# Wider key projections in a second attention layer, paired maxima and shifts, and row scaling on ScalarE

## The reference

```python
x = x + L0_xattn(ctx, layernorm(x), ctx, ...)        # 16 heads of 64, causal
x = x + L0_ffn(layernorm(x), gate, up, down)         # FP4-quantised, width 352
x = x + L1_xattn(layernorm(x), ctx, Wq, Wk, Wv, Wk_ip, Wv_ip, Wo, bo)
x = x + L1_ffn(layernorm(x), router, 8 experts, top 2)

# L1_xattn: two softmaxes over two segments of the keys, the outputs added
q = (x @ Wq);  k = ctx[:, :77] @ Wk;  k_ip = ctx[:, 77:] @ Wk_ip    # v, v_ip alike
out = softmax(q k^T / 8) v + softmax(q k_ip^T / 8) v_ip
out = out @ Wo + bo
```

## Time and profile before

| | us |
|---|---|
| median of 3 runs | 664.25 (664.08 to 667.1) |
| the profiled execution | 667.46 |
| its span, first to last instruction | 665.7 |
| first step of the second layer (scores of n = 64) | 248.3 |
| scores of n = 126 | 540.7 |
| VectorE copies the first expert's weights | 552.6 |
| mean granted TensorE clock | 0.978 |

### The profile page before, as it was taken

The page is one execution under the profiler, slowest core; times in us unless marked ns, Lnnn a source line. Parts: engine busy times, 40 slices in busy tenths (PEclk is TensorE's granted clock), DMA queues, the critical chain, the costliest instruction groups (busy, mean ns, idle before and its releaser), DMA issues.

```text
span 665.7 us, 16842 instructions
## 1 busy us (share of the span) xinstructions
PE 617.7 (93%) x5833; PEld 568.2 (85%) x5833; DVE 492.1 (74%) x1370; ACT 461.8 (69%) x1397; POOL 309.8 (47%) x444
## 2 busy tenths in 40 slices
PE   5898999999999999999999999999999987998990
PEld 5787888898888899999989989889888976988990
DVE  6578676586886869888898896888675675674654
ACT  5988999998888986656565656665663545665762
POOL 4365354354434444444444352445336575565550
PEclk9999999999999999999999999999897999998995
DMA  9800000000000000346654060000000001212215
GB/s 226 256 2 1 1 2 1 2 1 3 1 1 1 3 17 2 127 95 126 114 118 91 2 159 1 2 1 1 1 6 28 26 25 47 64 57 65 77 49 198
DMA packets 49612, 33.36 MB, mean 50 GB/s; under 512 B 9508, under 2 KB 46088, under 8 KB 49528
## 3 DMA queue, kind: packets, MB, share of 16 engines
q1 hardware_dynamic: 47256, 27.61, 16.8%
q0 software_dynamic: 2272, 4.67, 2.1%
HBM read 17.64 MB, written 14.63 MB: 48 GB/s over the span
## 4 chain that ended last, share of the span: by engine, by line
PE 64%; ACT 11%; issue 9%; POOL 7%; DVE 4%; DMA 3%; SPq 0%; POOLq 0%; DVEq 0%; ACTq 0%
PE ps_h L812 7%; PE ps_j L590 7%; PE ps_s L759 7%; ACT scores L987 7%; PE ps_t L797 6%; PE ps_h L829 6%; PE ps_j L369 5%; PE ps_j L371 4%; PE ps_j L370 4%; PE ph L1717 4%; PE py L1728 4%; POOL probs L1531 3%; POOL xs_scratch L1642 2%; PE pf L620 2%; PE pf L677 1%
## 5 line engine op out<-in xcount | busy, mean ns | idle before, releaser
L1531 POOL TENSOR_TENSOR probs<-scores,rsums 128x308 f32<-128x308 f32 (+1 forms) x192 | 153.5, 814 | 203.5 <-DVE rsums L1276 203.3
L987 ACT ACTIVATE scores<-scores,neg_max 128x128 f32<-128x128 f32 x256 | 99.8, 398 | 0.1
L956 ACT ACTIVATE probsT<-ps_t 128x512 f32<-128x512 f32 x128 | 76.3, 596 | 20.2 <-PE ps_t L797 19.8
L797 PE MATMUL ps_t<-ident,probs 128*128 128x128 f32 x512 | 78.4, 276 | 7.9 <-ACT probsT L956 4.3
L759 PE MATMUL ps_s<-KT,QT 64*128 64x128 f32 x1024 | 75.7, 288 | 0.8 <-ACT KT L859 0.8
L853 ACT ACTIVATE QT<-ps_j 128x512 f32<-128x512 f32 x64 | 38.1, 596 | 52.4 <-PE ps_j L371 52.4
L812 PE MATMUL ps_h<-probsT,V 128*64 128x128 f32 x1024 | 70.3, 279 | 1.4 <-DVE x_sb L1031 1.4
L759 PEld LDWEIGHTS ps_s<-KT,QT 64*128 64x128 f32 x1024 | 63.3, 190 | 8.7 <-issue 2.4
L829 PE MATMUL ps_h<-Wo,headsT 128*128 128x128 f32 x512 | 67.8, 275 | 1.7 <-ACT headsT L949 1.7
L797 PEld LDWEIGHTS ps_t<-ident,probs 128*128 128x128 f32 x512 | 58.7, 141 | 12.5 <-POOL probs L1531 8.3
L812 PEld LDWEIGHTS ps_h<-probsT,V 128*64 128x64 f32 x1024 | 55.0, 137 | 12.4 <-issue 11.1
(11 more groups left out here) (241 smaller groups left out, 1682.8 us busy)
## 6 DMA issues: line engine op xcount, KB each, us to landing
xs_scratch<-xs SPq DMA_DIRECT2D x8, 1032.0 KB, 7.7
xt<-xs_scratch SPq DMA_DIRECT2D x39, 64.5 KB, 1.8
w1b<-in_L_ffn_w_dram SPq DMA_DIRECT2D x1, 2048.0 KB, 8.2
big_raw<-in_L_ffn_w_dram SPq DMA_DIRECT2D x8, 256.0 KB, 4.8
ysum<-y_scratch SPq DMA_DIRECT2D x4, 512.0 KB, 5.3
Wo<-in_L_xattn_Wo_dram SPq DMA_DIRECT2D x2, 512.0 KB, 4.5
out_dram<-x_sb SPq DMA_DIRECT2D x4, 256.0 KB, 2.4
x_sb<-in_x_dram SPq DMA_DIRECT2D x3, 256.0 KB, 8.8
```

The lines of the kernel that those rows point to most:

```text
L797: ins = nc.tensor.transpose(ps_pT[:, j * S:(j + 1) * S], probs[s % 2][:, j, :], ident[:, :])
L956: nc.scalar.activation(probsT[(s - 2) % 4][:, :, :].rearrange("p h s -> p (h s)"), ps_pT[:, :], ACT.Copy).then_inc(SS["pT_copied"], 1)
L987: ins = nc.scalar.activation(scores[s % 4][:, j, :], scores[s % 4][:, j, :], ACT.Exp, bias=neg_max[:, s % 4, 0, j:j + 1], accum_out=sums[: ...
L1531: ins = nc.gpsimd.tensor_tensor(probs[(s - 1) % 2][:, :, k0:k1], scores[r][:, :, k0:k1], rsums[:, r, i, :].rearrange("p (h a) -> p h a", a ...
```

## The change

1. **Keys.** In the second layer `project_k` makes the keys of two groups (four batches) at once, for a block in every other group: for even blocks in groups 0, 2, 4, 6, for odd blocks alone in group 0, in pairs in groups 1, 3, 5, alone in group 7. The second group's keys go to a new home `KT_next`, the last 2048 columns of `big_raw`. A matmul now has 308 or 204 columns, and each of the two tiles fills a bank of its own: tile 0 bank 0, tile 1 bank 1, which is the bank of Q. So TensorE waits for the copy of Q between the tiles, also where a block is made alone. V has bank 0.
2. **Maxima and shifts.** The two score banks become one tensor of 1024 columns, `scores` one tensor; VectorE takes the maxima of both steps in one reduction for each segment, and shifts both steps in one addition for each segment. The semaphore `shifted` rises by 2 behind the last one.
3. **Scaling on ScalarE.** The last product of the norms A, C and D (D but for the last group) goes to ScalarE, two activations of 128x128 with a scale from SBUF: A in slot 3, C in slot 4 behind the tanh, D one step later than before, at the head of ScalarE's step.
4. **Expert weights.** The second half of `w2b`, which now lies under `KT_next`, is loaded after the last scores.

The diff, cut (comments, renamed arguments and repeated hunks left out):

```diff
+        KT_next = big_raw[:, L1_COLS - BLOCKS * TILES * PAIR * S:L1_COLS].rearrange(
+            "p (h t b s) -> p h t b s", h=BLOCKS, t=TILES, b=PAIR)
...
-        scores = [sbuf(f"scores{i}", [P, HB, S], F32, mem) for i in range(4)]
+        scores_all = sbuf("scores", [P, 4, HB, S], F32, mem)
+        scores = [scores_all[:, i, :, :] for i in range(4)]
...
-        ps_scores = psum_banks(["ps_s0", "ps_s1"], mem)
+        ps_pair = mem.enter_context(nc.psum_tensor("ps_s", [P, 2 * 512], F32))
+        ps_scores = [ps_pair[:, par * 512:(par + 1) * 512] for par in range(2)]
...
+        def k_groups(m):
+            g, hb = m % (GROUPS * BLOCKS) // BLOCKS, m % BLOCKS
+            if m < GROUPS * BLOCKS or hb % 2 == 1 and g == 0:
+                return [g]
+            if g % 2 == hb % 2:
+                return [g, g + 1] if g + 1 < GROUPS else [g]
+            return []
+
+        def k_upto(m):
+            return min(m, GROUPS * BLOCKS) + sum(TILES for i in range(GROUPS * BLOCKS, m) if k_groups(i))
+
+        def q_bank(m):
+            return ps_proj[(3 * (m % BLOCKS) + 1) % 2 if m < GROUPS * BLOCKS else 1]
+
+        def k_bank(m, t):
+            return ps_proj[(3 * (m % BLOCKS)) % 2 if m < GROUPS * BLOCKS else t]
+
+        def v_bank(m):
+            return ps_proj[(3 * (m % BLOCKS)) % 2 if m < GROUPS * BLOCKS - 1 else 0]
+
+        def k_home(m):
+            return KT[m % BLOCKS % 2] if k_groups(m) else KT_next[:, m % BLOCKS, :, :, :]
...
             def project_q(m, g, hb, lay):
-                wait_pos(pe, SS["k_copied"], m)
+                wait_pos(pe, SS["k_copied"], k_upto(m))
+                if lay == 1:
+                    pe.wait_ge(SS["q_copied"], m)
...
             def project_k(m, g, hb, lay):
+                groups = k_groups(m)
+                if not groups:
+                    return
...
                 for t in range(TILES):
+                    bank = k_bank(m, t)
+                    if lay == 1 and t == 1:
+                        pe.wait_ge(SS["q_copied"], m + 1)
                     for (k0, k1), w in zip(SEGS[lay], WK[lay]):
...
+                            of = slice(g, g + len(groups))
+                            dst = bank[:, :].rearrange("p (g c) -> p g c", g=2)[:, 0:len(groups), k0 * PAIR:k1 * PAIR]
+                            hi, lo = (c[:, of, k0:k1, :].rearrange("p g s b -> p g (s b)") for c in (ctxT_hi, ctxT_lo))
+                        ins = three_pass(pe, dst, w, cols, hi, lo)
+                    if lay == 1:
+                        ins.then_inc(SS["k_ready"], 1)
...
             def project_v(m, G, hb, lay, last):
...
-                pe.wait_ge(SS["q_copied"], m + 1 + (not last))
+                if m < GROUPS * BLOCKS - 1:
+                    pe.wait_ge(SS["q_copied"], m + 2)
+                else:
+                    pe.wait_ge(SS["v_copied"], m)
+                    if not last and k_groups(m + 1):
+                        pe.wait_ge(SS["k_copied"], k_upto(m + 1) + 1)
...
             def copy_k(m, hb):
...
+                homes = [KT[hb % 2], KT_next[:, hb, :, :, :]][0:len(k_groups(m))]
+                for t in range(TILES if homes else 0):
+                    act.wait_ge(SS["k_ready"], k_upto(m) + t + 1)
+                    for i, home in enumerate(homes):
+                        ins = nc.scalar.activation(
+                            home[:, t, :, :],
+                            k_bank(m, t)[:, i * PAIR * S:(i + 1) * PAIR * S].rearrange("p (s b) -> p b s", b=PAIR),
+                            ACT.Copy)
+                    ins.then_inc(SS["k_copied"], 1)
...
+            def scale_rows(g, which, dst, src, name):
+                act.wait_ge(SS["rstd" + name], 2 * g + 2)
+                for b in range(PAIR):
+                    ins = nc.scalar.activation(dst[:, b, :], src[:, b, :], ACT.Copy,
+                                               scale=frstd[:, which, b:b + 1])
+                ins.then_inc(SS["xn" + name], 1)
...
+                if s == 3 and n is not None:
+                    scale_rows(n, 0, fx, fx, "A")
...
+                if s == 4 and c is not None:
+                    scale_rows(c, 1, fy, fy, "C")
...
+                if fd["s"] == 7 and fd["d"] < GROUPS - 1:
+                    scale_rows(fd["d"], 2, xs[0][:, fd["d"] * PAIR:(fd["d"] + 1) * PAIR, 0:D], fz, "D")
...
-                    if at == (6, 2):
+                    if at == (6, 2) and d == GROUPS - 1:
...
+            def pair_max(s, i):
+
+                k0, k1 = SEGS[1][i]
+                nc.vector.tensor_reduce(pair_of(neg_max[:, i, :, :], s).rearrange("p t h -> p (t h)"),
+                                        pair_bank()[:, :, k0:k1], AX_X, ALU.max,
+                                        negate=True).then_inc(SS["max_ready"], 1)
...
+            def shifted_pair(n, s):
+
+                wait_pos(dve, SS["probs_ready"], n - 2)
                 for i, (k0, k1) in enumerate(SEGS[1]):
+                    dve.wait_ge(SS["max_ready"], n + i + 1)
+                    ins = nc.vector.tensor_tensor(
+                        scores_all[:, s % 4:s % 4 + 2, :, k0:k1].rearrange("p t h k -> p (t h) k"),
+                        pair_bank()[:, :, k0:k1],
+                        pair_of(neg_max[:, i, :, :], s).rearrange("p t (h a) -> p (t h) a", a=1)
+                        .broadcast_to([P, 2 * HB, k1 - k0]), ALU.add)
+                ins.then_inc(SS["shifted"], 2)
...
-                        dve.wait_ge(SS["scores_ready"], n + 1)
-                        row_max(s, bank_of(0), lay)
+                        dve.wait_ge(SS["scores_ready"], n + 2)
+                        pair_max(s, 0)
                         if has_sums:
                             invert_sums(n, p4, before)
-                        dve.wait_ge(SS["scores_ready"], n + 2)
-                        row_max(s + 1, bank_of(1), lay)
-                        for par in range(2):
-                            shifted_scores(n + par, s + par)
+                        pair_max(s, 1)
+                        shifted_pair(n, s)
...
-            dve.wait_ge(s_w2, 16 * (E + 1))
+            dve.wait_ge(s_w2, 16 * (E + 2))
...
+            for part in range(2):
+                if part == 1:
+                    sp.wait_ge(SS["scores_ready"], NG * STEPS)
+                es = slice(part * E // 2, (part + 1) * E // 2)
+                for e in range(es.start, es.stop):
...
```

77 lines of the change are left out of this document (35 added, 42 removed).

## The result

The changed kernel takes 661.85 us (median of 20 executions, 655.73 to 664.58) against 664.26 (20 executions, 662.11 to 667.1). That is 2.4 us less by the medians and 3.0 us by the means; the ratio, which goes by means, is 0.9954, interval 0.9936 to 0.9971. The forecast was 657.8: the direction is right and the time lies inside the range, but the change is worth about a third of what I summed. Two later comparisons gave 0.9988 (0.9963 to 1.0012) and 1.0002 (0.9968 to 1.0035), that is, nothing.

A forecast was written before the change was run, and what follows sets the result against it. TensorE's work was taken to bound the kernel from the second layer's first step to 540 us. -14.3 + 5.8 + 1.4 - 0.7 + 0.5 + 0.8 = -6.5 us gave 657.8 us, range 651.5 to 663 (8 in 10).

The forecast's parts named there:

- a difference carries over to the median: In the sum: the -6.5 us made on the profiled execution (667.46) also holds from the median, 664.25 to 657.75.
- Keys, the work: Second layer's key matmuls on TensorE: 14 pairs of blocks save 1.02 us each, -14.3 us (-12.0 to -17.9).
- rival 4: Second layer's keys: a wide matmul costs two narrow ones, the 14.3 us are gone; +7.8, time 672; chance 0.04.
- Keys, the new wait: Second layer: TensorE waits for ScalarE's copy of Q between key tiles, in 18 blocks; +5.8 us (+3 to +9).
- What comes late next: Second layer's blocks without keys: probabilities sometimes late for transposes, 0.1 us for each of 14; +1.4 us (0 to +6).
- rival 2: Second layer: each block without keys misses its probabilities by 0.4 us; sum -2.3, time 662; chance 0.20.
- Maxima and shifts: VectorE, pairs of steps: fusing takes 0.24 us a pair off, the first Exp is later; -0.7 us (-3 to +2).
- scaling: Products moved to ScalarE: +0.5 us, three first-layer groups against VectorE's relief; +0.8 us for D at step 127.
- that sign: Trunk's end: the first expert copy stays as far behind the last scores as before, about 11 us.
- Expert weights: Half load after the last scores, landing by 551, before VectorE needs them at 552.64; at nothing, +1 at worst.
- The stretches: Second layer up to the last scores 5 to 9 us shorter than 292; first layer changes by 2 at most.
- Rival 3: Second layer: ScalarE late with Q's copy at each of 18 waits; at 0.8 us +7.9, time 672; chance 0.07.

The follow-up runs named there:

- one bank: The changed kernel with single blocks' two key tiles in one bank, copied at once without waiting for Q: ratio 0.9950, 2.9 us faster than the changed kernel.
- a second kernel: Router's three fills added to the kernel with single blocks' key tiles in one bank and pairs' second tile behind the transposes: 656.5 against 659.4 us, ratio 0.9892.

## Why the prediction was wrong, and where it was right

**The failed step** is a sentence of the sum, "a difference carries over to the median", and the one behind it that let the clock stand at 1.00 "in all stretches of rows 2". The difference of -6.5 us about holds at equal clock: -6.8 and -5.2 of span x clock in two comparisons, -6.8 and -6.1 between the few executions of equal clock. The term that is missing is the clock: +6.0 us of lost clock in both. In time it is nearer 5 us, an estimate from the fills, which gave 4.3 us for 0.0074 of the 0.009. That the two profiled executions (0.978 and 0.975) differ by the very sum is partly luck, because the clock of the one before was low for its kernel. Rows 2 showed three stretches with a full clock; between them, from 475 to 515 us, the profile of the kernel before had it fall twice, and I did not read that stretch. There the saving was also mis-told: "a block without keys reaches its transposes 1.27 us sooner" leaves out that at steps 116, 118 and 122 it reaches the router's matmuls sooner, whose products are not ready. That wait took the place of the work, and brought the clock down with it: three waits of about 0.9 us ahead of the router's matmuls, filled with 0.84 us of work each, moved the mean clock by 0.0074. The Trainium skill's rule on idle gaps (TensorE: Matmul & The Clock Gate, Why this matters for your kernels) was used in the prediction to put the clock aside, with "No stall above comes near it"; that shorter waits are safe does not follow from it, and the measurement says that these were not.

Point by point, by the prediction's own steps:

- **Keys, the work** (-14.3 us): distances 0.14 and 0.11, as taken. Right. The reading by columns alone, rival 4, falls.
- **Keys, the new wait** (+5.8): in a pair 0.10 + 0.11 = 0.21 against 0.19 + 0.05; the parts were off, the sum right. A pair with its wait costs 1.70 us where 1.76 was forecast. In the second layer's first two blocks it is 2.2 us more than before where my terms give 0.99 + 0.86 = 1.85.
- **What comes late next** (+1.4): four of eleven blocks without keys missed by 0.31 to 0.74 us, 1.8 us in all by step 114, and no wait of TensorE for probabilities over 0.5 us up to 535 us. Right for the probabilities. With the router's 2.7 us of waits, which the term left out, it is 4.5 us, 0.32 in each of 14 blocks. That is close to rival 2's 0.4 and its 662 us is the time measured, but its mechanism falls: what came late was not the probabilities, and most of the time was lost through the clock.
- **Maxima and shifts** (-0.7) and **scaling** (+0.5, +0.8): 0.26 us a pair off VectorE, estimated 0.24. VectorE is busy 89.6% of the stretch, not 88% or less. Together +1.1 of span x clock alone and -1.5 beside the keys, so they lie on both sides of my +0.6; that this goes by how full TensorE is was not tested. The scaling at step 127 delayed Exp by 8.03 - 6.76 = 1.3 us behind the last scores (1.9 forecast) and the first expert copy by 1.1 (547.73, 13.1 us behind the last scores, 11.9 before), so that sign did not hold; undone, it gave nothing.
- **Expert weights** (0): issued from 535.90 to 538.0, hidden; nothing waits for them by name in the trace, and VectorE's idle time ahead of its first expert copy is 1.45 us where it was 1.58.
- **The stretches**: the first layer changed by 0.37 us (under 2 forecast), the second up to its last scores by -7.9 from step 64 on, 292.4 to 284.5 (-5 to -9 forecast). The 1.5 us between, the block of step 62 with the second layer's first keys, are in neither; counted up to step 64 the first stretch is 1.9 us longer. Both signs held, and they could not show what the clock does from one execution to the next.
- **Rival 3** (ScalarE late with Q): a 1.13 us wait in the first pair, 0.42 in the block behind, none listed elsewhere up to 535 us. It falls.

**What stays open:** why one bank gained more clock than work, how much of the falls at the trunk's end and in the expert stage can be had back, and the last 1.0 us of lost clock with the router filled.

## What to carry to other kernels

A saving on an engine that stands in dense work is worth its trace value only if the clock is the same afterwards: compare the mean granted clock over many executions on one chip, not two profiles, before a difference is carried over. Where work is taken out ahead of an instruction that waits for another engine, ask first whether the wait will simply take its place; if it will, leave the work there, or put useless matmuls in the wait, once profiles of the same chip show that the wait is there. Read the clock in every stretch of the page, above all where it is not full.

## What the hardware showed that I had not expected

Twenty-one useless matmuls, 2.5 us of work in three waits, gave 4.3 us (0.9722 to 0.9796 in mean clock), and 3.0 us in a second kernel, though not each wait that TensorE has costs it clock. Matmuls too narrow to save time by their width still take nearly twice as long at the lower level. The kernel before, keys of a tile at a clock of 0.50:

```profile
481.63 0.33 PE L369 MATMUL ps_j<-ctxT_hi,l_lo 128*128 128x154 f32 x1
...
482.36 0.41 PE L370 MATMUL ps_j<-ctxT_lo,l_hi 128*128 128x102 f32 x1
482.57 0.34 PE L371 MATMUL ps_j<-ctxT_hi,l_hi 128*128 128x102 f32 x1
482.75 0.30 PE L369 MATMUL ps_j<-ctxT_hi,l_lo 128*128 128x154 f32 x1
```

Two matmuls of 102 columns stand 0.21 apart, and the six of the tile take 1.12 us (481.63 to 482.75) where 12 take 1.27 at full clock. And the kernel before's mean clock differs little from chip to chip (0.9811 to 0.9826 on four) while its time differs by 4 us, so ratios must come from one chip.
